# Attention denominators from partial sums and raw tiles, and quads of denominators in the linear stage

## The chip, the cores and the metric

The kernel runs on one core of a Trainium2 chip. The metric is the device time of one execution in microseconds (us); three executions of the kernel before took 5260.36, 5265.98 and 5267.3 us, a median of 5265.98.

## The reference

Two layers follow each other on an image of 512 channels and 64 x 64 points (4096 tokens).

```
# layer 0
qn = group_norm(x); vn = group_norm(qn)
q, k, v = conv1x1(qn, wq, bq), conv1x1(vn, wk, bk), conv1x1(vn, wv, bv)
attn = softmax(einsum('bhnd,bhmd->bhnm', q, k) * scale)     # 16 heads of 32
out  = conv1x1(einsum('bhnm,bhmd->bhnd', attn, v), wo, bo)
x    = (out + x) / sqrt(2)
# layer 1
qkv    = einsum('oc,bchw->bohw', w_qkv, x)
qkv_ms = concat([qkv, pointwise(depthwise5x5(qkv))])
out    = vk @ q, with vk = [v, 1] @ relu(k)^T and q = relu(q)   # 64 heads of 8, both halves
out    = out[:, :, :-1] / (out[:, :, -1:] + 1e-15)
out    = batch_norm(einsum('oc,bchw->bohw', w_proj, out)) + x
```

## The kernel before

Five stages run one after another, each a function with a program for every engine: `stage_qkv`, `stage_attention`, `stage_output`, `stage_linear` and `stage_project`. The change touches three of them.

**Attention.** A unit is one head with 1024 queries; there are 64. The 32 key tiles of a unit are taken in 16 pairs, and four pairs (eight tiles) make an octet, so that there are 256 octets. For each pair TensorE issues four score matmuls (L643), each followed by one of the matmuls of `max_product` (L630), which find the row maxima of the next unit. ScalarE exponentiates the scores into `prob` (L779), a ring of two octets; VectorE reads the maxima out of a ring of four PSUM banks (`read_max`, L806). After every second pair comes `times_v` (L656) for two older pairs. In the fourth pair of an octet, ahead of its last maximum, stands `denominators` (L666) for the octet before: matmuls with a column of ones over two sums of tiles, one result row per half and sum in a PSUM bank of the same ring. Once in a unit the maxima are turned (`transpose_shift`, L637).

The two sums of an octet come from GpSimd and VectorE. GpSimd (`eight_steps`, L606 and L612) adds tiles 0 to 3 into the first sum, and tiles 6 and 7 onto the second, whose first addition, tiles 4 and 5, is VectorE's (`add`, L825). The addition stands on VectorE ahead of the last maximum of the octet, and GpSimd waits for it. ScalarE reads the denominators (`read_den`, L745) ahead of an octet's first exponential. What orders the work is the program written out for each engine; the engines meet at semaphores alone.

**Linear stage.** A tile T is one role (K, V or Q) of one group of 128 channels; there are 12 tiles of 8 chunks, and one step s per chunk. A step multiplies by the weights into one PSUM bank (`conv1`, L1253), which ScalarE reads twice. After the eighth step comes `conv5` (L1269), a burst of 400 matmuls of 32 x 32 that makes the 5 x 5 part of four chunks; the other four come from VectorE's `dsum` (L1439, L1442), through one matmul each (`mix`, L1280). Pieces of kind "c" come from `conv1`, pieces "x" from the 5 x 5 part; the x pieces of tile T are read during tile T+1, four by `read_conv5` (four activations each, L1361) and four by `read_mix` (one activation, L1367). Each piece is then posted: K and V pieces are transposed (L1301), Q pieces are multiplied into a numerator (L1294) and into 16 denominator rows (L1296), both read by ScalarE (L1377, L1379) and stored. A Q piece is posted three steps after it is made (`LAG`). The next `conv5` waits for all x pieces of the tile before (`x_read`).

**Project stage.** It loads the denominators, inverts them on VectorE (`invert`, L1586), stores the inverses (`store_inverse`, L1501), loads them back spread over the heads (L1521), divides (L1594) and multiplies by the weights (L1549).

Of the kernel before, what the change touches and what calls it, by code (L numbers as in the profile page):

```python
# [38 lines left out]
class Scratch:  # L39


    def __init__(self, nc):
# [6 lines left out]
        self.den = nc.dram_tensor("scratch_den", (2, GROUPS, HPG, N), F32, kind="Internal").ap()  # L49
# [294 lines left out]
def stage_attention(nc, x, scr, v_tok, x1, x_in, ident_d):  # L344
# [14 lines left out]
    ADDS = 5  # L359
# [20 lines left out]
    with ExitStack() as ctx:  # L380
# [34 lines left out]
        dve_added = sem("b_dve_added")  # L415
# [12 lines left out]
        counted = (*k_in, *q_in, v_in, shift_in, scored, exped, times_v_done, dve_added, pool_added,  # L428
# [169 lines left out]
        def _(pool):  # L598
            def eight_steps(g, b):

                p = prob[:, b * OCT:(b + 1) * OCT, :]
                a_, b_ = sums[:, b, 0, :], sums[:, b, 1, :]
# [21 lines left out]
        def _(pe):  # L624
# [177 lines left out]
        def _(dve):  # L802
# [36 lines left out]
            def turn(i, final):  # L839
                for u, head, par, c in units(i):  # L840
                    place = par * UNITS + c
                    for pair in range(PAIRS):
# [6 lines left out]
                        for n in range(PER_PAIR):  # L849
                            if n == PER_PAIR - 1 and pair % (OCT // 2) == OCT // 2 - 1:  # L850
                                o = pair // (OCT // 2)
                                add(u * OCTS + o, o % 2)
# [198 lines left out]
def stage_linear(nc, w_all, dw_all, pw_all, mask_d, heads_d, ident_d, scr, x1):  # L1051

    ALONE = 4
# [5 lines left out]
    LAG = {K: 1, V: 1, Q: 3}  # L1061
    RING = 4
    OUT_RING = 4
    BLK = P // 4
# [22 lines left out]
    for s in range(STEPS):  # L1087
        for kind in "xc":
            for i in posts_at[s][kind]:
                parts = (("num", 0), ("den", 1)) if role_of(i) == Q else (("tr", 1 if kind == "x" else 0),)  # L1090
# [5 lines left out]
    final = {(kind, i): number[kind, i, "den" if role_of(i) == Q else "tr"] for kind, i in PIECES}  # L1096
    v_order = [p for s in range(STEPS) for p in times_at[s]]
    v_number = {p: n for n, p in enumerate(v_order)}
    q_order = sorted((p for p in PIECES if role_of(p[1]) == Q), key=lambda p: number[(*p, "den")])
    q_number = {p: n for n, p in enumerate(q_order)}  # L1100

# [6 lines left out]
    with ExitStack() as ctx:  # L1108
# [12 lines left out]
        bd = sb("d_bd", [P, 2, P])  # L1121
# [9 lines left out]
        den_w = sb("d_den_w", [P, 2, HPG])  # L1131
        num = sb("d_num", [P, OUT_RING, BANK])
        den = sb("d_den", [HPG, OUT_RING, BANK])
# [24 lines left out]
        stored = [sem(f"d_stored{i}") for i in range(OUT_RING)]  # L1158
        block = ctx.enter_context(nc.Block())

        @block.sync
        def _(sp):
# [16 lines left out]
            def store(kind, i):  # L1179
                q, n, at = q_number[kind, i], chunk_of(kind, i), part_of(kind)  # L1180
                r = q % OUT_RING
                sp.wait_ge(post_read, number[kind, i, "den"] + 1)
# [512 lines left out]
```

## Time and profile before

| | us |
|---|---|
| median of three runs | 5265.98 |
| the profiled execution, own time | 5261.72 |
| its span in the trace | 5259.9 |
| TensorE busy | 4970.8 (95%) |
| VectorE busy | 4297.0 (82%) |
| GpSimd busy | 3101.7 (59%) |
| ScalarE busy | 2902.8 (55%) |

The span begins with the program's first instruction and ends with its last. Attention takes it from about 336 us to 3872 us, the linear stage from 4019 to 4971 us, the project stage the rest. Busy time of TensorE counts matmuls whose ends are modelled, so that one which starts late for a wait can still look covered; the starts of the instructions are what to read.

### The profile page before, as it was taken

The page shows a single profiled execution, that of the slowest core. Times are in us where ns is not written, and L with a number is a line of the kernel's source. Part 1 is how long each engine was busy: PE and PEld are TensorE (multiplying, and loading weights), DVE is VectorE, ACT ScalarE, POOL GpSimd, SP SyncE. Part 2 cuts the span into 40 slices and gives each one's busy share as a digit, 9 for nine tenths or more (in the row PEclk, how much of TensorE's full clock was granted, in tenths as well). Part 3 has the DMA queues.
Part 4 walks back from the last instruction along what each step waited for, and adds up shares of the span by engine and source line. Part 5 has one row for each costly group of instructions (what it writes and reads, how often), then busy time and mean ns, then how long its engine had stood idle before and what let it go on. Part 6 is the DMA issues. An engine that isn't in the chain of part 4 may idle for free. (4 is left out here: it accounts for less than half of the span.)

```text
span 5259.9 us, 100067 instructions
## 1 busy us (share of the span) xinstructions
PE 4970.8 (95%) x32432; PEld 2650.2 (50%) x32432; DVE 4297.0 (82%) x5145; ACT 2902.8 (55%) x5349; POOL 3101.7 (59%) x1336
## 2 busy tenths in 40 slices
PE   7989999999999999999999999999978999999797
PEld 6854444444444444444444444444435555555343
DVE  4359999999999999999999999999946878678533
ACT  2216666666666666666666666666641443443302
POOL 0008888888888888888888888888840000000000
PEclk9979999999999999999999999999989999999998
DMA  4330000100001010010100101011031010000254
GB/s 155 128 101 12 24 17 24 28 13 24 17 24 28 14 27 14 24 29 12 29 12 24 29 12 29 12 27 61 22 126 38 16 34 16 31 25 23 94 155 155
DMA packets 103338, 221.24 MB, mean 42 GB/s; under 512 B 13776, under 2 KB 23120, under 8 KB 100176
## 3 DMA queue, kind: packets, MB, share of 16 engines
q1 hardware_dynamic: 102864, 215.00, 13.0%
q8 instruction: 288, 4.72, 0.4%
q14 instruction: 186, 1.52, 0.1%
HBM read 132.64 MB, written 81.79 MB: 41 GB/s over the span
## 5 line engine op out<-in xcount | busy, mean ns | idle before, releaser
L612 POOL TENSOR_TENSOR b_sums<-b_sums,b_prob 128x1024 f32<-128x1024 f32 x1024 | 2440.0, 2383 | 432.5 <-DVE b_sums L825 284.7
L806 DVE TENSOR_REDUCE b_mx<-b_pmax 128x1 f32<-128x512 f32 x4096 | 2504.8, 679 | 213.7 <-PE b_pmax L630 211.8
L779 ACT ACTIVATE b_prob<-b_pscore 128x512 f32<-128x512 f32 x4096 | 2174.2, 610 | 483.1 <-PE b_pscore L643 476.0
L630 PE MATMUL b_pmax<-b_kst,b_qst 96*128 96x512 f32 x4096 | 1808.3, 445 | 107.1 <-DVE b_mx L806 91.2
L643 PE MATMUL b_pscore<-b_qst,b_kst 98*128 98x512 f32 x4096 | 1636.8, 400 | 16.1 <-DMA b_qst<-b_mlow 11.8
L630 PEld LDWEIGHTS b_pmax<-b_kst,b_qst 96*128 96x128 f32 x4096 | 781.9, 191 | 1012.1 <-DVE b_mx L806 667.1
L656 PE MATMUL b_pout<-b_prob,b_vst 128*32 128x512 f32 x8192 | 991.9, 602 | 0.0
L643 PEld LDWEIGHTS b_pscore<-b_qst,b_kst 98*128 98x128 f32 x4096 | 780.5, 191 | 154.4 <-ACT b_prob L779 25.0
L606 POOL TENSOR_TENSOR b_sums<-b_prob 128x1024 f32<-128x1024 f32 x256 | 612.7, 2393 | 390.6 <-ACT b_prob L779 386.2
L825 DVE TENSOR_TENSOR b_sums<-b_prob 128x1024 f32<-128x1024 f32 x256 | 789.0, 3082 | 43.0 <-ACT b_prob L779 43.0
L1442 DVE SCALAR_TENSOR_TENSOR d_dsum<-d_ypad,d_dw,d_dsum 128x2048 f32<-128x2048 f32 x288 | 681.9, 2368 | 10.2
L656 PEld LDWEIGHTS b_pout<-b_prob,b_vst 128*32 128x32 f32 x8192 | 214.5, 109 | 487.4 <-issue 283.1
L745 ACT ACTIVATE b_outd<-b_pmax 128x512 f32<-128x512 f32 x256 | 153.2, 598 | 554.8 <-PE b_pmax L666 424.1
L1225 POOL TENSOR_TENSOR d_num_w<-d_vks,d_mask 128x128 f32<-128x128 f32 x8 | 3.6, 456 | 762.6 <-ACT d_vks L1403 762.6
L1253 PE MATMUL d_pmain<-v_tok,d_w 128*128 128x512 f32 x768 | 351.7, 601 | 17.7 <-DVE d_tv_x L1426 11.0
L1269 PE MATMUL d_pdw<-d_ypad,d_wtap 32*32 32x512 f32 x9600 | 312.9, 599 | 3.2 <-ACT d_piece_x L1367 2.4
L1361 ACT ACTIVATE d_piece_x<-d_pdw 32x512 f32<-32x512 f32 x192 | 113.0, 589 | 310.4 <-PE d_pdw L1269 307.8
L666 PE MATMUL b_pmax<-b_sums,b_ones 128*1 128x512 f32 x2048 | 266.9, 593 | 2.8 <-POOL b_sums L612 2.8
L1269 PEld LDWEIGHTS d_pdw<-d_ypad,d_wtap 32*32 32x32 f32 x9600 | 214.1, 103 | 96.4 <-issue 18.3
L1549 PE MATMUL f_ps<-f_num,f_w 128*128 128x512 f32 x512 | 223.0, 599 | 35.6 <-DVE f_num L1594 35.6
L1253 PEld LDWEIGHTS d_pmain<-v_tok,d_w 128*128 128x128 f32 x768 | 138.8, 191 | 185.4 <-issue 175.3
L1439 DVE TENSOR_SCALAR d_dsum<-d_ypad,d_dw 128x2048 f32<-128x2048 f32 x12 | 15.4, 1287 | 217.6 <-ACT d_piece_c L1354 217.6
(159 smaller groups left out, 2422.3 us busy)
## 6 DMA issues: line engine op xcount, KB each, us to landing
b_kst<-scratch_kh SPq DMA_DIRECT2D x32, 512.0 KB, 10.6
b_qst<-scratch_qh SPq DMA_DIRECT2D x128, 128.0 KB, 2.9
scratch_att<-b_outn SPq DMA_DIRECT2D x128, 128.0 KB
scratch_num<-d_num SPq DMA_DIRECT2D x64, 256.0 KB, 2.0
f_num<-scratch_num SPq DMA_DIRECT2D x8, 2048.0 KB, 10.1
f_rden<-scratch_rden SPq DMA_DIRECT2D x64, 256.0 KB, 9.5
v_tok<-in_x SPq DMA_DIRECT2D x8, 1024.0 KB, 12.7
scratch_qh<-a_high SPq DMA_DIRECT2D x8, 1024.0 KB, 4.2
```

The lines of the kernel that those rows point to most:

```text
L606: pool.tensor_tensor(a_, p[:, 0, :], p[:, 1, :], ALU.add).then_inc(pool_added, 1)
L612: pool.tensor_tensor(acc, acc, p[:, step, :], ALU.add).then_inc(pool_added, 1)
L630: pe.matmul(pmax[bank][:], qst[0:SUMS, b, t * P:(t + 1) * P], kst[0:SUMS, par, j * BANK:(j + 1) * BANK], start=True, stop=True).then_inc(m ...
L643: pe.matmul(pscore[score_bank(hs)][:], kst[0:FULL, par, kt * P:(kt + 1) * P], qst[0:FULL, b, at], start=True, stop=True).then_inc(scored, 1)
L656: mm = pe.matmul(pout[row:row + HD, :], vst[:, par, kt, :], prob[:, kt % PBUF, half * BANK:(half + 1) * BANK], start=(pair == 0), stop=(pa ...
L666: mm = pe.matmul(pmax[bank][row:row + 1, :], ones[:], sums[:, o % 2, s, half * BANK:(half + 1) * BANK], start=True, stop=True)
L779: act.activation(prob[:, kt % PBUF, half * BANK:(half + 1) * BANK], pscore[score_bank(hs)][:], ACT.Exp, scale=SCALE).then_inc(exped, 1)
L806: dve.tensor_reduce(mx[:, b, t, j:j + 1], pmax[bank][:], AX.X, ALU.max).then_inc(max_read, 1)
L825: dve.tensor_tensor(sums[:, b, 1, :], prob[:, b * OCT + 4, :], prob[:, b * OCT + 5, :], ALU.add).then_inc(dve_added, 1)
L1253: mm = pe.matmul(pmain[:], w[:, b, k, :], x1[:, k, n * BANK:(n + 1) * BANK], start=(k == 0), stop=(k == KC - 1))
L1269: mm = pe.matmul(pdw[r][c * BLK:(c + 1) * BLK, :].rearrange("p (r c) -> p r c", c=IMG), wtap[rows, b, tap, :], ypad[rows, b, y:y + ROWS, d ...
L1442: add = dve.scalar_tensor_tensor(acc, src, dw[:, b, tap:tap + 1], acc, ALU.mult, ALU.add)
```

## The change

In attention, GpSimd makes both sums alone, each of three tiles (0 to 2, 3 to 5), in four additions; tiles 6 and 7 are not added. `denominators` has eight matmuls: four over the sums, and four that accumulate the raw tiles 6 and 7 from `prob` onto the same rows. VectorE's addition is gone. In the linear stage a Q piece gives a numerator alone; after every fourth piece one bundle of four matmuls makes the denominators of all four pieces, in four strips of 32 rows of one bank. ScalarE reads them at once, VectorE inverts them there, and SyncE stores the inverses where the project stage reads them. The four `mix` matmuls of a tile become one bundle of sixteen matmuls of 32 x 32, and its results are read by `read_conv5`, in four activations each. `LAG` of Q is 2 instead of 3, the ring of pieces 6 instead of 4. The project stage has no inversion and no store of inverses.

```diff
-    ADDS = 5
+    ADDS = 4
+    RAW = 6
...
                 pool.wait_ge(den_done, done(g - 1))
-                pool.wait_ge(exped, done((g * OCT + 2) * 2))
-                pool.tensor_tensor(a_, p[:, 0, :], p[:, 1, :], ALU.add).then_inc(pool_added, 1)
-                for n, (acc, step) in enumerate(((a_, 2), (a_, 3), (b_, 6), (b_, 7))):
-                    pool.wait_ge(pool_added, done(g * ADDS + n + 1))
-                    pool.wait_ge(exped, done((g * OCT + step + 1) * 2))
-                    if n == 2:
-                        pool.wait_ge(dve_added, done(g + 1))
-                    pool.tensor_tensor(acc, acc, p[:, step, :], ALU.add).then_inc(pool_added, 1)
+                for s in range(2):
+                    at = 3 * s
+                    pool.wait_ge(exped, done((g * OCT + at + 2) * 2))
+                    pool.tensor_tensor(sums[:, b, s, :], p[:, at, :], p[:, at + 1, :], ALU.add).then_inc(pool_added, 1)
+                    pool.wait_ge(pool_added, done(g * ADDS + 2 * s + 1))
+                    pool.wait_ge(exped, done((g * OCT + at + 3) * 2))
+                    pool.tensor_tensor(sums[:, b, s, :], sums[:, b, s, :], p[:, at + 2, :],
+                                       ALU.add).then_inc(pool_added, 1)
...
                 pe.wait_ge(pool_added, done((u * OCTS + o + 1) * ADDS))
-                for half in range(2):
-                    for s in range(2):
-                        row = (half * 2 + s) * HD
-                        mm = pe.matmul(pmax[bank][row:row + 1, :], ones[:],
-                                       sums[:, o % 2, s, half * BANK:(half + 1) * BANK],
-                                       start=True, stop=True)
+                pe.wait_ge(exped, done((u * OCTS + o + 1) * OCT * 2))
+                for raw in range(2):
+                    for half in range(2):
+                        for s in range(2):
+                            row = (half * 2 + s) * HD
+                            terms = prob[:, o % 2 * OCT + RAW + s, :] if raw else sums[:, o % 2, s, :]
+                            mm = pe.matmul(pmax[bank][row:row + 1, :], ones[:],
+                                           terms[:, half * BANK:(half + 1) * BANK],
+                                           start=(raw == 0), stop=(raw == 1))
                 mm.then_inc(den_done, 1)
...
-            def add(g, b):
-
-                dve.wait_ge(den_done, done(g - 1))
-                dve.wait_ge(exped, done((g * OCT + 6) * 2))
-                dve.tensor_tensor(sums[:, b, 1, :], prob[:, b * OCT + 4, :], prob[:, b * OCT + 5, :],
-                                  ALU.add).then_inc(dve_added, 1)
...
-    LAG = {K: 1, V: 1, Q: 3}
-    RING = 4
+    LAG = {K: 1, V: 1, Q: 2}
+    RING = 6
...
+            def store_quad(kind, i):
+                q, at = quad_number[kind, i], part_of(kind)
+                row = (at * GROUPS + group_of(i)) * HPG
+                sp.wait_ge(inverted, q + 1)
+                for c in range(QUAD):
+                    n = chunk_of(kind, i - QUAD + 1 + c)
+                    sp.dma_start(scr.rden[row:row + HPG, n * BANK:(n + 1) * BANK],
+                                 den[c * BLK:c * BLK + HPG, q % 2, :]).then_inc(den_stored[q % 2], 16)
...
-                pe.matmul(pdw[n][:], bd[:, T % 2, :], dsum[:, T % 2, n * BANK:(n + 1) * BANK],
-                          start=True, stop=True).then_inc(l_done, 1)
+                for r in range(4):
+                    rows = slice(r * BLK, (r + 1) * BLK)
+                    for c in range(ALONE):
+                        mm = pe.matmul(pdw[r][c * BLK:(c + 1) * BLK, :], bdq[rows, b, :],
+                                       dsum[rows, b, c * BANK:(c + 1) * BANK], start=True, stop=True)
+                mm.then_inc(l_done, 1)
...
-                    free(number[kind, i, "den"])
-                    pe.matmul(ppost[1][0:HPG, :], den_w[:, at, :], mine, start=True, stop=True).then_inc(post_done, 1)
+                    if i % QUAD == QUAD - 1:
+                        free(number[kind, i, "den"])
+                        for c in range(QUAD):
+                            mm = pe.matmul(ppost[1][c * BLK:(c + 1) * BLK, :], den_w[:, at, :],
+                                           piece[kind][:, (i - QUAD + 1 + c) % RING, :], start=True, stop=True)
+                        mm.then_inc(post_done, 1)
...
-                c = i % CHUNKS
-                act.wait_ge(burst_done, i // CHUNKS + 1)
+                c = i % SUPER
+                if i % CHUNKS < SUPER:
+                    act.wait_ge(burst_done, i // CHUNKS + 1)
+                else:
+                    act.wait_ge(l_done, i // CHUNKS + 1)
                 out = slot("x", i)
                 for r in range(4):
                     last = act.activation(out[r * BLK:(r + 1) * BLK, :], pdw[r][c * BLK:(c + 1) * BLK, :], func(i))
                 last.then_inc(x_read, 1)
...
-                act.activation(slot("x", i), pdw[n][:], func(i)).then_inc(x_read, 1)
...
+            def invert(kind, i):
+                dve.wait_ge(post_read, number[kind, i, "den"] + 1)
+                at = den[:, quad_number[kind, i] % 2, :]
+                dve.reciprocal(at, at).then_inc(inverted, 1)
...
-                dve.reciprocal(dens[:, 1, at], dens[:, 0, at]).then_inc(inverted, 1)
```

TensorE in attention, at the end of an octet (`b_pout` are the values, `b_pmax` the ring of maxima and denominators), before and then with the change:

```order
L643 MATMUL b_pscore<-b_qst,b_kst 128x512
L656 MATMUL b_pout<-b_prob,b_vst 32x512 x8
L666 MATMUL b_pmax<-b_sums,b_ones 1x512 x4
L630 MATMUL b_pmax<-b_kst,b_qst 128x512
L643 MATMUL b_pscore<-b_qst,b_kst 128x512
```

```order
L642 MATMUL b_pscore<-b_qst,b_kst 128x512
L655 MATMUL b_pout<-b_prob,b_vst 32x512 x8
L668 MATMUL b_pmax<-b_sums,b_ones 1x512 x4
L668 MATMUL b_pmax<-b_prob,b_ones 1x512 x4
L629 MATMUL b_pmax<-b_kst,b_qst 128x512
L642 MATMUL b_pscore<-b_qst,b_kst 128x512
```

Four matmuls over `prob` stand behind the four over `b_sums`; nothing else has moved there.

VectorE in attention, at the same place (`b_mx` takes the maxima), before; with the change the middle three rows are absent and the reads follow each other:

```order
L805 REGISTER_ALU
L806 TENSOR_REDUCE b_mx<-b_pmax 128x1
L823 REGISTER_ALU
L824 ISA
L825 TENSOR_TENSOR b_sums<-b_prob 128x1024
L805 REGISTER_ALU
L806 TENSOR_REDUCE b_mx<-b_pmax 128x1
```

TensorE in the linear stage, two steps of a Q tile and what stands at their ends (`d_pmain` is `conv1`, `d_pvk` the values times keys, `d_pdw` with `d_dsum` the mix), before and then with the change:

```order
L1253 MATMUL d_pmain<-v_tok,d_w 128x512 x4
L1313 MATMUL d_pvk<-d_tv_x,d_tk 128x129 x4
L1301 MATMUL d_ppost<-d_ident,d_piece_x 128x128 x4
L1280 MATMUL d_pdw<-d_dsum,d_bd 128x512
L1294 MATMUL d_ppost<-d_piece_c,d_num_w 128x512
L1296 MATMUL d_ppost<-d_piece_c,d_den_w 16x512
L1269 MATMUL d_pdw<-d_ypad,d_wtap 32x512 x400
```

```order
L1308 MATMUL d_pdw<-d_dsum,d_bdq 32x512 x16
L1323 MATMUL d_ppost<-d_piece_c,d_num_w 128x512
L1279 MATMUL d_pmain<-v_tok,d_w 128x512 x4
L1346 MATMUL d_pvk<-d_tv_x,d_tk 128x129 x4
L1334 MATMUL d_ppost<-d_ident,d_piece_x 128x128 x4
L1323 MATMUL d_ppost<-d_piece_c,d_num_w 128x512
L1327 MATMUL d_ppost<-d_piece_c,d_den_w 32x512 x4
L1279 MATMUL d_pmain<-v_tok,d_w 128x512 x4
```

The first piece shows the last step of a tile, in which mix and denominator stand between the transposes and the burst. In the second, the mix of a whole tile stands in its fifth step, the denominators of four pieces in the sixth; the last step has neither.

## Rows read from the trace of the kernel before

**Rows 1.** Busy time by stretch: PE, PEld, DVE, ACT, POOL; then PEclk, DMA share, GB/s.

```profile
1000.00:2000.00 1000.00, 970.35 (x5304) 489.02 (x5307) 938.70 (x1286) 681.80 (x1290) 872.46 (x368) 1.00 0.08 22
3836.00:3850.00 14.00, 13.27 (x60) 4.19 (x56) 3.69 (x2) 8.54 (x17) 13.18 (x6) 0.87 0.00 1
4200.00:4973.00 773.00, 758.66 (x9709) 416.22 (x9708) 565.15 (x243) 323.08 (x575) 45.11 (x41) 1.00 0.09 29
```

**Rows 2.** Timeline of TensorE, one unit of attention (start us, us, engine, line, names, count).

```profile
2014.30 1.04 PE L666 MATMUL b_pmax<-b_sums,b_ones 128*1 128x512 f32 x8
...
2040.84 1.04 PE L666 MATMUL b_pmax<-b_sums,b_ones 128*1 128x512 f32 x8
2041.81 0.50 PE L630 MATMUL b_pmax<-b_kst,b_qst 96*128 96x512 f32 x1
...
2046.84 1.92 PE L656 MATMUL b_pout<-b_prob,b_vst 128*32 128x512 f32 x16
2048.70 0.50 PE L630 MATMUL b_pmax<-b_kst,b_qst 96*128 96x512 f32 x1
...
2052.62 1.92 PE L656 MATMUL b_pout<-b_prob,b_vst 128*32 128x512 f32 x16
2054.36 1.04 PE L666 MATMUL b_pmax<-b_sums,b_ones 128*1 128x512 f32 x8
...
2062.34 0.50 PE L630 MATMUL b_pmax<-b_kst,b_qst 96*128 96x512 f32 x1
...
2066.93 1.92 PE L656 MATMUL b_pout<-b_prob,b_vst 128*32 128x512 f32 x16
2068.67 1.04 PE L666 MATMUL b_pmax<-b_sums,b_ones 128*1 128x512 f32 x8
```

**Rows 3.** Timeline of VectorE in the octet that begins at 2040.84.

```profile
2040.50 3.24 DVE L825 TENSOR_TENSOR b_sums<-b_prob 128x1024 f32<-128x1024 f32 x1
...
2049.24 4.88 DVE L806 TENSOR_REDUCE b_mx<-b_pmax 128x1 f32<-128x512 f32 x8 [0.71 <-PE b_pmax L630]
```

**Rows 4.** Costliest groups: VectorE's and GpSimd's sums, scores, the 5 x 5 burst.

```profile
L825 DVE TENSOR_TENSOR b_sums<-b_prob 128x1024 f32<-128x1024 f32 x256 | 789.0, 3082 | 43.0 <-ACT b_prob L779 43.0
L612 POOL TENSOR_TENSOR b_sums<-b_sums,b_prob 128x1024 f32<-128x1024 f32 x1024 | 2440.0, 2383 | 432.5 <-DVE b_sums L825 284.7
L643 PE MATMUL b_pscore<-b_qst,b_kst 98*128 98x512 f32 x4096 | 1636.8, 400 | 16.1 <-DMA b_qst<-b_mlow 11.8
L1269 PE MATMUL d_pdw<-d_ypad,d_wtap 32*32 32x512 f32 x9600 | 312.9, 599 | 3.2 <-ACT d_piece_x L1367 2.4
```

**Rows 5.** Timeline of TensorE, linear stage, last step of a Q tile: mix, numerator, denominator, burst.

```profile
4440.18 1.02 PE L1280 MATMUL d_pdw<-d_dsum,d_bd 128*128 128x512 f32 x2
4441.03 1.02 PE L1294 MATMUL d_ppost<-d_piece_c,d_num_w 128*128 128x512 f32 x2
4441.99 1.03 PE L1296 MATMUL d_ppost<-d_piece_c,d_den_w 128*16 128x512 f32 x2
4442.95 1.13 PE L1269 MATMUL d_pdw<-d_ypad,d_wtap 32*32 32x512 f32 x31
```

**Rows 6.** Timeline of ScalarE in that step: the V piece read.

```profile
4440.38 0.60 ACT L1396 ACTIVATE d_tv_x<-d_ppost 128x512 f32<-128x512 f32 x1 [0.24 <-PE d_ppost L1301]
```

**Rows 7.** Timeline of ScalarE in an earlier step of that tile: a 5 x 5 piece read.

```profile
4396.83 2.39 ACT L1361 ACTIVATE d_piece_x<-d_pdw 32x512 f32<-32x512 f32 x4
```

**Rows 8.** Chain of waits at the start of the project stage.

```profile
4973.86 2.81 DMA f_proj<-scratch_den
4976.70 3.36 DVE f_proj L1586
4980.08 9.69 DMA scratch_rden<-f_proj
```

**Rows 9.** DMA issues of the numerators (count, KB each, median us to landing).

```profile
f_num<-scratch_num SPq DMA_DIRECT2D x8, 2048.0 KB, 10.1
```

More of the change, by code:

```diff
@@ L1095, in stage_linear, with inverted_before @@
                     latest[bank] = n
-    final = {(kind, i): number[kind, i, "den" if role_of(i) == Q else "tr"] for kind, i in PIECES}
+    final = {(kind, i): number[kind, i // QUAD * QUAD + QUAD - 1, "den"] if role_of(i) == Q
+             else number[kind, i, "tr"] for kind, i in PIECES}
     v_order = [p for s in range(STEPS) for p in times_at[s]]
     v_number = {p: n for n, p in enumerate(v_order)}
-    q_order = sorted((p for p in PIECES if role_of(p[1]) == Q), key=lambda p: number[(*p, "den")])
+    q_order = sorted((p for p in PIECES if role_of(p[1]) == Q), key=lambda p: number[(*p, "num")])
     q_number = {p: n for n, p in enumerate(q_order)}
+    quads = [p for p in q_order if p[1] % QUAD == QUAD - 1]
+    quad_number = {p: n for n, p in enumerate(quads)}
+    def inverted_before(kind, i):
+        return min(main_step(kind, i) // CHUNKS + 1, TILES)
+    quads_before = {T: [p for p in quads if inverted_before(*p) == T] for T in range(TILES + 1)}
+    quads_after = {T * CHUNKS + ALONE: quads_before[T] for T in range(TILES)}
+    quads_after[TILES * CHUNKS + ALONE] = [p for p in quads_before[TILES] if p[0] == "c"]
+    quads_after[STEPS] = [p for p in quads_before[TILES] if p[0] == "x"]
     def group_of(i):
@@ L1158, in stage_linear @@
         stored = [sem(f"d_stored{i}") for i in range(OUT_RING)]
+        den_stored = [sem(f"d_den_stored{i}") for i in range(2)]
+        inverted = sem("d_inverted")
         block = ctx.enter_context(nc.Block())
@@ L1193, in _ @@
                     load(T + 1)
+                for p in quads_after.get(s, ()):
+                    store_quad(*p)
                 for kind in "xc":
@@ L1197, in _ @@
                             store(kind, i)
+            for p in quads_after[STEPS]:
+                store_quad(*p)
             for r in range(OUT_RING):
-                sp.wait_ge(stored[r], len(range(r, len(q_order), OUT_RING)) * 32)
+                sp.wait_ge(stored[r], len(range(r, len(q_order), OUT_RING)) * 16)
+            for r in range(2):
+                sp.wait_ge(den_stored[r], len(range(r, len(quads), 2)) * 16 * QUAD)
         @block.gpsimd
@@ L1324, in _ @@
                 x = s - CHUNKS
-                if 0 <= x < LAST and x % CHUNKS >= SUPER:
-                    mix(x)
+                if 0 <= x < LAST and x % CHUNKS == SUPER:
+                    mix(x // CHUNKS)
                 for i in posts_at[s]["c"]:
@@ L1422, in _ @@
         def _(dve):
+            dve.memset(den_w[:], 0.0).then_inc(zeroed, 1)
             for b in range(2):
@@ L1443, in _ @@
                     add.then_inc(dlink, 1)
+            for p in quads_before[TILES]:
+                invert(*p)
 def stage_project(nc, wprojT, chan_bn, scr, x1, out):
@@ L1472, in stage_project @@
         ps = [ctx.enter_context(nc.psum_tensor(f"f_ps{i}", [P, BANK], F32)) for i in range(8)]
-        den_in = [sem(f"f_den_in{i}") for i in range(2)]
-        inverted = sem("f_inverted")
-        inv_out = [sem(f"f_inv_out{i}") for i in range(2)]
         w_in = sem("f_w_in")
@@ L1496, in _, with turn @@
                 sp.sem_inc(s, CREDIT)
[L1498 to L1504 removed]
             sp.dma_start(w[:], wprojT.rearrange("(m p) o -> p m o", p=P)).then_inc(w_in, 16)
             sp.dma_start(par[:], chan_bn).then_inc(w_in, 16)
[L1507 removed]
+            def turn(i):
                 for b in range(2):
@@ L1522, in turn @@
                                          .to_broadcast([HPG, GH, BANK])).then_inc(rden_in[part], 16)
-                    if not final:
-                        store_inverse(n + 2, b)
-            store_inverse(0, 0)
-            store_inverse(1, 1)
-            with sp.Fori(0, CHUNKS // 2 - 1) as i:
-                turn(i, False)
-            turn(CHUNKS // 2 - 1, True)
+            with sp.Fori(0, CHUNKS // 2) as i:
+                turn(i)
             for t in range(KC):
```

80 lines of the change are left out of this document (31 added, 49 removed).

## Prediction

> **What bounds the kernel now.** I read the busy time by stretch first, since the share over the whole span mixes stages. In attention TensorE is busy 970 of 1000 us and VectorE 939, ScalarE only 682 [rows 1]: two engines are nearly full, and the page does not tell which waits for which. The timeline of TensorE tells it [rows 2]. An octet has two runs of sixteen score and maximum matmuls. The second goes from 2048.70 to 2052.62, 3.92 us; the first, of the same instructions, from 2041.81 to 2046.84, 5.03 us. On VectorE its addition runs from 2040.50 for 3.24 us [rows 3]: no maximum is read meanwhile, the ring of four banks fills, and TensorE stands. Behind the second run VectorE had been idle 0.71 us and reads eight maxima in 4.88 us [rows 3], slower than TensorE's 3.92, but the ring carries the lag and the matmuls behind the run (1.86 us or more) let it catch up.
>
> So without the addition TensorE's own octet is 3.92 + 1.86 (2046.84 to 2048.70) + 3.92 + 1.74 (2052.62 to 2054.36) + 0.97 (2040.84 to 2041.81, denominators) = 12.41 us. The run with the turn takes 4.59 instead of 3.92 (2062.34 to 2066.93), since the turn takes a bank of the ring; I count those 0.67 us as staying. A unit is 4 x 12.41 + 0.67 = 50.31 us of TensorE's own. It took 54.37 (2014.30 to 2068.67) [rows 2]. **4.06 us a unit are stalls from VectorE's addition.**
>
> In the linear stage TensorE goes from instruction to instruction [rows 5], except where ScalarE is late; the project stage starts behind a chain of transfers [rows 8].
>
> **The change, part by part.**
>
> *VectorE's addition goes.* It is 256 x 3.08 us [rows 4], but on the path it is worth the stalls alone: -4.06 us a unit, if all go. VectorE then needs two times 4.88 us for an octet's maxima, some 10 us with the turn's small reads, against 13.3 of TensorE (below). What is late next is TensorE itself.
>
> *Four more denominator matmuls an octet.* They are of the same form as the four that stand there, in the same four strips. No row shows eight in a row; the bounds are 0.86 us, half of the 1.74 that two groups of `times_v` take, and 0.97, what a denominator group takes with the change back to scores [rows 2]. That change comes once an octet whatever the group's length, so 0.86 is nearest: +3.44 us a unit. TensorE's octet becomes 13.27 us. The new wait for all exponentials of the older octet is for work that ended four pairs earlier. ScalarE reads denominators 0.86 us later relative to the last run, but the next scores come later by as much; it is busy 682 of 1000 us and gets no more to do [rows 1].
>
> *GpSimd* goes from five additions to four, 4 x 2.38 [rows 4], under 10.2 us with its gaps, and no longer waits for VectorE. It is covered by TensorE's 13.27.
>
> *A rule that speaks against this.* An addition costs VectorE 3.08 us and GpSimd 2.38 [rows 4]. The Trainium skill (GPSIMD Engine Reference, Engine selection) would put an elementwise addition on VectorE, GpSimd being about two times slower with two inputs. The trace differs: run beside GpSimd's, VectorE's addition is the dearer one, and the measurement decides. By the rule the addition would take VectorE some 1.2 us, an estimate from its factor and the 2.38; most of the stall would have another cause and stay, and the time would be that of rival A.
>
> Over the 63 units that have maxima, -4.06 + 3.44 = -0.62 gives **-39 us**. The last unit has none and no such stall: four groups of 0.86 us, **+3**. The scores wait 11.8 us in all for a row of shifts that is loaded [rows 4], at units' starts, right behind a denominator group; a group 0.86 us longer hides part, between 0 and 7 us; I take **-4**.
>
> *Linear stage, TensorE.* A denominator takes 0.96 us, a mix 0.85 [rows 5]. Of 64 denominators 53 lie ahead of the last burst, and become 13 bundles; a bundle is four matmuls in four strips, bounded by 0.86 and by 0.97 as above; I take 0.96: -40 x 0.96 = -38. Of 48 mixes 44 become 11 bundles of 16 matmuls, 32 instructions at the burst's 312.9/9600 us [rows 4], 1.04: -44 x 0.85 + 11 x 1.04 = -26.
>
> *Given back in the last step of a tile.* The burst waits until the last x piece is read. Today that read is one activation behind a short mix, done by the time numerator and denominator are through: the burst starts at 4442.95 [rows 5]. Now it is four activations, 2.39 us [rows 7]. ScalarE begins the V piece at 4440.38 [rows 6], can begin the four 0.5 us later, ends them at 4443.3, and the burst starts near 4443.4; TensorE, without mix and denominator, would be through at 4441.1. That is 2.2 us of wait here, 2.6 to 2.9 in K and V tiles, which have less to do on TensorE there; between 0 (were ScalarE ahead) and 2.9. I take 2.6, eleven times: +29. The other steps hold: ScalarE is busy 323 of 773 us there [rows 1], and 144 more activations less 48 denominator reads, at 0.6 us (2.39/4), make that 381.
>
> VectorE's sixteen inversions, 3.36 us each [rows 8], two at a tile's start, fall into its waits: it is busy 565 of the 773 us [rows 1], with them some 620 of 735. Were that cover gone, they would cost up to 54 us. The part after the last burst is bound by ScalarE; it loses eight denominator reads and gains a last inversion and four stores: -3, between -8 and +4. Linear stage: -38 - 26 + 29 - 3 = **-38 us**.
>
> *Project stage.* Load, inversion and store of the first inverses go, 2.81 + 3.36 + 9.69 = 15.9 us [rows 8], the most that can be won. Under them lay the weights (2 MB) and the first numerators (2 MB, 10.1 us to land [rows 9]); now these stand in the open. If both must land one after the other, some 20 us from the same start, about 5 us are won. I take the middle, **-10 us**.
>
> **Sum.** -39 + 3 - 4 - 38 - 10 = -88. Against the profiled execution's own 5261.7 us that is 5174. The median of the three runs stands 4.3 us above that execution; I let this lie within the range.
>
> **The rivals.**
>
> *A. The maxima still hold TensorE: slower.* VectorE reads a maximum in 0.61 us (4.88/8), TensorE makes one in 0.47; if the first run stays behind the second's pace even without the addition, for instance because the ring is one bank short while denominators lie in it longer, part of the 4.06 us stays while the 3.44 are paid in full. It decides at a third: if more than 1.4 us (88/63) a unit stay, nothing is won in the whole kernel. With half staying, +128: 5302 us. For it: the turn's run is held by just that, one bank less. Against it: the second run follows 1.86 us behind the first, and shows no stall. 8 in 100, and 3 more for a third staying (5259).
>
> *B. The clock.* In an octet of the last unit the granted clock is 0.87 of 2.4 GHz instead of 1.00 [rows 1], in a stretch where TensorE stands idle between short pieces: part of it ran at 1.2 GHz. Should the longer stretch of denominators, which fill one column in 32 of the array, do that to every octet, 0.13 x 14 = 1.8 us come on top each time, 466 in all: 5640. Against it: the present group and the bursts of the linear stage keep the clock at 1.00 [rows 1], and idle time falls. 3 in 100.
>
> *C. The linear stage gives nothing,* because ScalarE, with 144 more activations, binds its other steps as well: 5212, still faster. For it: a burst already waits for it. Against it: half its time there is idle. 9 in 100.
>
> *D. More is won:* the turn's 0.67 us go too (-42), or the burst does not wait (-29): about 5120. 7 in 100.
>
> **How the numbers follow.** The forecast as summed has 70 in 100, and lies within 5135 to 5215 by the bounds of its terms (28 us for 0.97 instead of 0.86 in attention, 8 in the linear stage, 6 in the project stage, up to 29 if bursts do not wait). With C, and part of D and of A's milder case, the range is 5130 to 5230. A difference under 0.2% (10.5 us) is about what a measurement of this kernel cannot tell from none. Faster by more than that: the forecast, C and D, 86; slower: A with half staying and B, 11; between: A's milder case, 3.
>
> **What would show it.** Right: no addition on VectorE in attention, runs of 3.9 us in both halves of an octet, octets of 13.3 us, units near 53.8, GpSimd idle over a fifth of attention, granted clock 1.00; sixteen inversions in the linear stage; bursts waiting for a read of 5 x 5 pieces by ScalarE; the first division about 10 us earlier after the stage begins. Wrong: first runs above 4.2 us (A), a granted clock under 0.95 in attention (B), steps of the linear stage that wait for ScalarE elsewhere (C). A unit above 54.4 us would refute the core.

## The result and the profile after

The changed kernel takes 5228.33 us (median of three, 5226.27 to 5231.29) against 5265.98: ratio 0.9929, interval 0.9915 to 0.9942. It is faster, by 37.7 us where 92 (against that median) were forecast; inside the stated range, by 1.7 us, but 54 us short of the forecast. The profiled execution has 5231.29 us of its own and a span of 5229.4, 30.5 us under the span before. Where these went, from the same marks in both traces (first score, last attention matmul, first and last burst, first projection matmul):

| stretch | before | after | change | forecast |
|---|---|---|---|---|
| start to the first score | 381.4 | 380.9 | -0.5 | 0 |
| attention, to its last matmul on TensorE | 3490.6 | 3478.9 | -11.7 | -40 |
| to the first 5 x 5 burst | 187.6 | 191.4 | +3.8 | 0 |
| first burst to the end of the last | 877.7 | 854.0 | -23.7 | -35 |
| to the first projection matmul | 68.3 | 71.2 | +2.8 | -13 |
| to the end | 254.3 | 253.0 | -1.3 | 0 |

**Attention did what was said, in most of its units.** Busy time by stretch of the changed kernel (us, then PE, PEld, DVE, ACT, POOL; granted clock; DMA):

```profile
1000.00:2000.00 1000.00, 996.92 (x5902) 525.86 (x5895) 722.80 (x1210) 655.27 (x1289) 695.85 (x294) 0.99 0.08 22
4200.00:4900.00 700.00, 663.57 (x9684) 393.22 (x9666) 581.73 (x246) 337.94 (x594) 35.27 (x30) 0.99 0.08 26
```

VectorE falls from 939 to 723 of 1000 us and GpSimd is idle for 304; TensorE goes from 970 to 997 [rows 1]. TensorE's timeline of one octet:

```profile
2010.56 1.04 PE L668 MATMUL b_pmax<-b_prob,b_ones 128*1 128x512 f32 x8
2011.53 0.50 PE L629 MATMUL b_pmax<-b_kst,b_qst 96*128 96x512 f32 x1
...
2015.47 1.92 PE L655 MATMUL b_pout<-b_prob,b_vst 128*32 128x512 f32 x16
2017.33 0.50 PE L629 MATMUL b_pmax<-b_kst,b_qst 96*128 96x512 f32 x1
...
2021.27 1.92 PE L655 MATMUL b_pout<-b_prob,b_vst 128*32 128x512 f32 x16
2023.01 1.04 PE L668 MATMUL b_pmax<-b_sums,b_ones 128*1 128x512 f32 x8
2023.86 1.04 PE L668 MATMUL b_pmax<-b_prob,b_ones 128*1 128x512 f32 x8
2024.84 0.50 PE L629 MATMUL b_pmax<-b_kst,b_qst 96*128 96x512 f32 x1
```

The first run of sixteen (2011.53 to 2015.47) and the second (2017.33 to 2021.27) now take 3.94 us each, where the first had taken 5.03 [rows 2]. Eight denominator matmuls take 0.85 + 0.98. From one denominator group to the next it is 13.31 us, forecast 13.27. VectorE waits for TensorE ahead of every run instead of the reverse; its timeline there:

```profile
2012.07 4.88 DVE L808 TENSOR_REDUCE b_mx<-b_pmax 128x1 f32<-128x512 f32 x8 [2.86 <-PE b_pmax L629]
2017.87 4.88 DVE L808 TENSOR_REDUCE b_mx<-b_pmax 128x1 f32<-128x512 f32 x8 [0.92 <-PE b_pmax L629]
```

The median of 62 units, taken from the starts of their first denominator group, falls from 54.36 to 53.90 us (53.75 forecast).

**But one unit in eight does not.** The program loops over eight units. At six of its seven turns TensorE waits, and its clock halves behind some of the waits. TensorE's timeline at the second turn, and its busy time and granted clock (the number behind the count) in windows around it:

```profile
1244.55 1.04 PE L668 MATMUL b_pmax<-b_sums,b_ones 128*1 128x512 f32 x8
1245.40 1.04 PE L668 MATMUL b_pmax<-b_prob,b_ones 128*1 128x512 f32 x8
1246.38 0.49 PE L629 MATMUL b_pmax<-b_kst,b_qst 96*128 96x512 f32 x1
1248.03 0.49 PE L642 MATMUL b_pscore<-b_qst,b_kst 98*128 98x512 f32 x1 [1.16 <-DMA b_qst<-b_mlow]
```

```profile
1233.00:1238.00 5.00, 5.00 (x31) 1.00 0.01 3
1243.00:1248.00 5.00, 3.87 (x33) 1.00 0.05 11
1248.00:1253.00 5.00, 4.97 (x14) 0.67 0.03 8
1253.00:1258.00 5.00, 5.00 (x23) 0.65 0.00 0
```

The row of shifts lands late at this turn (a DMA), and TensorE stands 1.16 us; in the ten us from 1248 on the granted clock is 0.67 and 0.65, so part of them ran at 1.2 GHz. Of seven turn units the three with such a stretch behind the wait took 57.6 to 58.9 us, three without it 56.1 to 56.3, and one, the last, had no wait. Not every wait is for the row. TensorE's waits from 420 to 3790 us (us, times, longest; "issue" is a wait for no engine and no transfer that the profile shows):

```profile
PE b_pscore L642 <- issue: 5.0, 3, 1.9
PE b_pscore L642 <- DMA b_qst<-b_mlow: 2.5, 2, 1.4
PE b_pmax L629 <- DVE b_mx L808: 1.9, 1, 1.9
```

All six stand at turns. In the kernel before the turns cost as much (seven turn units together 19.0 us over the median), but the units right behind them were 13.0 us under it, 52.3 us instead of 54.4. There the denominator groups behind the second turn stand 12.45 and 12.67 us apart, where those ahead of it stand 13.55 apart; 12.45 is close to the 12.41 that the prediction had worked out as TensorE's own octet:

```profile
1222.42 1.04 PE L666 MATMUL b_pmax<-b_sums,b_ones 128*1 128x512 f32 x8
1235.97 1.04 PE L666 MATMUL b_pmax<-b_sums,b_ones 128*1 128x512 f32 x8
...
1268.15 1.04 PE L666 MATMUL b_pmax<-b_sums,b_ones 128*1 128x512 f32 x8
1280.60 1.04 PE L666 MATMUL b_pmax<-b_sums,b_ones 128*1 128x512 f32 x8
1293.27 1.04 PE L666 MATMUL b_pmax<-b_sums,b_ones 128*1 128x512 f32 x8
```

VectorE's additions there took 1.21 and 2.36 us, not 3.26 as in the median. So most of the addition's stall is absent for two octets, and the turn is in part made up. In the changed kernel the turn units are 20.0 us over their median and those behind them 0.3 over: nothing is made up.

**The linear stage has new waits.** TensorE's waits from the first burst to the end of the last, in the changed kernel, then before (us, times, longest):

```profile
PE d_pdw L1295 <- ACT d_piece_x L1397: 25.8, 11, 2.8
PE d_ppost L1334 <- ACT d_num L1408: 13.3, 15, 0.9
PE d_ppost L1334 <- ACT d_den L1414: 2.4, 3, 0.8
```

```profile
PE d_ppost L1301 <- ACT d_den L1379: 4.6, 6, 0.8
PE d_pdw L1269 <- ACT d_piece_x L1367: 2.4, 7, 0.3
```

The first line is the forecast wait for the last 5 x 5 piece; the second was not forecast. In the last step of a K tile, where x pieces of the Q tile before it are still to be multiplied (TensorE, then ScalarE):

```profile
4499.98 1.02 PE L1323 MATMUL d_ppost<-d_piece_x,d_num_w 128*128 128x512 f32 x2
4501.90 0.63 PE L1334 MATMUL d_ppost<-d_ident,d_piece_c 128*128 128x128 f32 x4 [0.90 <-ACT d_num L1408]
4504.33 2.25 PE L1295 MATMUL d_pdw<-d_ypad,d_wtap 32*32 32x512 f32 x58 [1.80 <-ACT d_piece_x L1397]
```

```profile
4501.15 0.60 ACT L1408 ACTIVATE d_num<-d_ppost 128x512 f32<-128x512 f32 x1
4501.78 2.40 ACT L1397 ACTIVATE d_piece_x<-d_pdw 32x512 f32<-32x512 f32 x4
```

A numerator (L1323) is followed by transposes (L1334) that use the same PSUM bank, so they wait until ScalarE has read it. Before, a denominator matmul of 0.96 us in the other bank stood between the two [rows 5]. And behind four of the burst waits the clock halved again. The burst of 800 matmuls with and without it, behind the same wait:

```profile
4122.62 27.62 PE L1295 MATMUL d_pdw<-d_ypad,d_wtap 32*32 32x512 f32 x800 [2.77 <-ACT d_piece_x L1397]
...
4579.04 26.08 PE L1295 MATMUL d_pdw<-d_ypad,d_wtap 32*32 32x512 f32 x800 [2.77 <-ACT d_piece_x L1397]
```

### The profile page after: what moved, and what is told of

Read it like the earlier page. It is cut to its first block and busy times, and to the rows that moved or that the text cites. A ratio compares the mean times of both kernels' runs of the same rounds, so it can differ in the third digit from the quotient of the medians.

```text
span 5229.4 us, 103029 instructions
## 1 busy us (share of the span) xinstructions
PE 4989.3 (95%) x34768; PEld 2766.3 (53%) x34768; DVE 3575.3 (68%) x4898; ACT 2878.2 (55%) x5445; POOL 2477.0 (47%) x1068
## 5 line engine op out<-in xcount | busy, mean ns | idle before, releaser
L781 ACT ACTIVATE b_prob<-b_pscore 128x512 f32<-128x512 f32 x4096 | 2089.8, 619 | 350.1 <-PE b_pscore L642 345.0
L607 POOL TENSOR_TENSOR b_sums<-b_prob 128x1024 f32<-128x1024 f32 x512 | 1220.7, 2384 | 1332.5 <-ACT b_prob L781 1332.5
L629 PE MATMUL b_pmax<-b_kst,b_qst 96*128 96x512 f32 x4096 | 1716.0, 422 | 17.9 <-DMA b_qst<-scratch_ql 15.2
L610 POOL TENSOR_TENSOR b_sums<-b_sums,b_prob 128x1024 f32<-128x1024 f32 x512 | 1220.5, 2384 | 89.7 <-POOL b_sums L607 86.7
L1397 ACT ACTIVATE d_piece_x<-d_pdw 32x512 f32<-32x512 f32 x384 | 226.3, 589 | 327.0 <-PE d_pdw L1295 313.9
L1295 PE MATMUL d_pdw<-d_ypad,d_wtap 32*32 32x512 f32 x9600 | 319.1, 610 | 26.7 <-ACT d_piece_x L1397 25.8
L668 PE MATMUL b_pmax<-b_prob,b_ones 128*1 128x512 f32 x2048 | 266.5, 592 | 0.0
L1577 PEld LDWEIGHTS f_ps<-f_num,f_w 128*128 128x128 f32 x512 | 98.0, 192 | 159.3 <-issue 159.3
```

Source lines behind the costliest of these rows:

```text
L607: pool.tensor_tensor(sums[:, b, s, :], p[:, at, :], p[:, at + 1, :], ALU.add).then_inc(pool_added, 1)
L610: pool.tensor_tensor(sums[:, b, s, :], sums[:, b, s, :], p[:, at + 2, :], ALU.add).then_inc(pool_added, 1)
L629: pe.matmul(pmax[bank][:], qst[0:SUMS, b, t * P:(t + 1) * P], kst[0:SUMS, par, j * BANK:(j + 1) * BANK], start=True, stop=True).then_inc(m ...
L668: mm = pe.matmul(pmax[bank][row:row + 1, :], ones[:], terms[:, half * BANK:(half + 1) * BANK], start=(raw == 0), stop=(raw == 1))
L781: act.activation(prob[:, kt % PBUF, half * BANK:(half + 1) * BANK], pscore[score_bank(hs)][:], ACT.Exp, scale=SCALE).then_inc(exped, 1)
L1295: mm = pe.matmul(pdw[r][c * BLK:(c + 1) * BLK, :].rearrange("p (r c) -> p r c", c=IMG), wtap[rows, b, tap, :], ypad[rows, b, y:y + ROWS, d ...
```

## Experiments

All times are medians; each was run beside the kernel before on the same chip (5263 to 5266 us).

**The two halves apart.** One kernel has `stage_attention` of the change and all else as before, the other the reverse.

```diff
-    ADDS = 5
+    ADDS = 4
+    RAW = 6
...
```

```diff
-    LAG = {K: 1, V: 1, Q: 3}
-    RING = 4
+    LAG = {K: 1, V: 1, Q: 2}
+    RING = 6
+    QUAD = 4
...
```

> The kernel before with the attention part of the change alone. By the prediction on record attention gains 40 us: about 5226 us. By the new theory (TensorE is now the bound of every unit, so the waits for the row of shifts at the loop's turns, one unit in eight, and the half clock behind them are paid in full, where the kernel before made them up in the next unit): units of 53.9 us, but 2 to 5 us more at a turn, 12 us won in all: about 5254 us.

> The changed kernel with attention as before, so the linear and project parts alone. By the prediction on record 48 us are won: about 5218 us. By the new theory about 20: the twelve bursts span 24 us less, the part behind the last burst takes 8 us more because numerators that follow each other in one bank each wait for ScalarE's read, the start of the project stage 5 us less: about 5246 us.

Measured: 5247.72 us (ratio 0.9970, 0.9959 to 0.9982), 16 won, near the new theory's 12 and far from 40; and 5235.40 us (0.9949, 0.9936 to 0.9963), 28 won, between the two. Both halves fell short, and attention by more.

**What the four matmuls cost, and who holds TensorE.**

```diff
-                for raw in range(2):
+                for raw in range(1):
...
-                                           start=(raw == 0), stop=(raw == 1))
+                                           start=True, stop=True)
```

> The changed kernel with the four denominator matmuls over unsummed tiles left out (tiles 6 and 7 of each octet are then not in the denominator). If TensorE alone sets the pace and four matmuls cost 0.86 us, a unit takes 53.87 - 3.44 = 50.4 us, attention 220 us less: about 5008 us. If the ring of maxima and VectorE's reads still hold TensorE (rival A of the prediction), a unit stays above 51.5 us: above 5075 us.

Measured: 5011.24 us, as the first theory said (this kernel leaves tiles 6 and 7 out of the denominators). The median unit is 50.47 us, 3.43 under the changed kernel's 53.90, so a group of four costs 0.86 us, the figure taken; and 50.47 is close to the 50.31 us that the prediction had worked out as TensorE's own. Rival A is refuted: without the addition TensorE's waits for VectorE come to 2.7 us in the whole of attention. The turn units are 17.4 us over the median here too.

**The turn of the loop.** The same edit in the changed kernel and in the kernel before:

```diff
-    EARLY = 2
+    EARLY = 3
```

> The changed kernel with the shifts made three pairs of key tiles before a unit's end instead of two, so that the row is loaded some 3 us earlier. By the new theory the waits of 1.2 to 1.9 us at the loop's turns and the half clock behind them go: 15 to 21 us less than the changed kernel, about 5210 us. By its rival (TensorE is late at the turn for its own instructions, and the row is only the last thing named) nothing changes: 5228 us.

> The kernel before with the shifts made three pairs before a unit's end instead of two, the same edit that took 20 us off the changed kernel. By the theory of lost slack the unit behind a loop's turn made up most of what the turn cost (52.3 us instead of 54.4), so little is to be won: 0 to 8 us, about 5260 us. By its rival (the edit is worth the same wherever TensorE waits at a turn) 15 to 20 us: about 5246 us.

Measured: 5208.18 us in the changed kernel, 20 under it; 5260.32 us in the kernel before (ratio 0.9997, 0.9988 to 1.0006), no change that can be told. The same edit is worth 20 us where TensorE is the bound, and nothing that can be told where VectorE's addition paced it. How slack absorbs it can be read in the kernel before: with the edit the median octet with the turn of the shifts takes 14.13 us instead of 14.30, and the next one 13.02 instead of 12.88. The new theory was wrong in one respect. TensorE's waits in attention (420 to 3790 us) with the edit:

```profile
PE b_pscore L642 <- issue: 5.0, 5, 1.2
PE b_pmax L629 <- DVE b_mx L808: 4.2, 6, 2.0
```

The wait for the row is gone, but waits for no engine and no transfer ("issue", 5.0 us before the edit too) stay at the turns, and reads of maxima come late behind them. Six turn units are still 2.2 to 3.9 us over the median: of the 18.9 us that attention gains, the turns give 5.0 (two of the three stretches at 1.2 GHz are gone). The most, 11.8, is the median unit, 53.71 instead of 53.90 us, because the octet with the turn of the shifts takes 13.80 instead of 13.96; which no theory had held. What remains of the theory is what the pair of runs shows, that the kernel before absorbed the edit. What holds TensorE at the turn stays open.

**Who is late at the burst.** ScalarE's reads of the mixed pieces but the first move to the head of a step, under the convolution's matmuls:

```diff
-                if 0 <= x < LAST and x % CHUNKS < SUPER:
+                if 0 <= x < LAST and x % CHUNKS != SUPER:
                     read_conv5(x)
...
-                if 0 <= x < LAST and x % CHUNKS >= SUPER:
+                if 0 <= x < LAST and x % CHUNKS == SUPER:
                     read_conv5(x)
```

> The changed kernel with the last three of the four mixed x pieces of a tile read by ScalarE at the head of a step, under the convolution's matmuls, instead of behind the step's other reads. If the order of ScalarE's reads in a tile's last step is what the burst waits for, the 25.8 us of waits go and with them the half clock behind some of them (four times 3.4 us): 26 to 33 us less, about 5199 us. If ScalarE is short of time in that step whatever its order, half of it at most: about 5215 us.

Measured: 5207.41 us, 21 won. First burst to the end of the last takes 832.4 us instead of 854.0, and no burst waits for a piece and no clock halves there any more. The 25.8 us of waits and 6 us of half clock are gone, and 10.8 come back in other waits, these and 2.3 us more for reads of values:

```profile
PE d_ppost L1334 <- ACT d_num L1408: 17.9, 18, 1.5
PE d_pmain L1279 <- ACT d_piece_c L1387: 4.9, 6, 1.0
```

**Numerators in two banks.**

```diff
-                    parts = (("num", 0), ("den", 1))
+                    parts = (("num", int(kind == "x")), ("den", int(kind == "c")))
...
-                    pe.matmul(ppost[0][:], num_w[:, at, :], mine, start=True, stop=True)
+                    pe.matmul(ppost[int(kind == "x")][:], num_w[:, at, :], mine, start=True, stop=True)
...
```

> The changed kernel with numerators of x pieces in the second bank and those of c pieces in the first (denominators in the other one each time), so that a numerator is no longer followed in its own bank by the next transposes or numerator of the same step. If the missing denominators had kept these apart, the 13.3 us of waits of transposes for numerators go, and the 8 us that the part behind the last burst took more: 15 to 21 us less, about 5210 us. If ScalarE's reads set the pace there whatever the bank, at most 5 us: 5224 us.

Measured: 5220.94 us (ratio 0.9920, 0.9907 to 0.9934), 7 won: nearer to the rival, and hardly clear of noise, since the changed kernel's interval is 0.9915 to 0.9942. The waits of transposes for numerators are gone, but TensorE only comes sooner to the burst:

```profile
PE d_pdw L1295 <- ACT d_piece_x L1397: 29.1, 11, 2.9
```

That line stood at 25.8 before the edit; a granted clock under 1.00 in the burst, four times in the changed kernel, comes seven times. So the shared bank was the cause of these waits, but behind them stood the same late reads. The part behind the last burst went from 71.2 to 69.8 us only, so the bank does not explain its lengthening.

**All three, and the last tile.** One kernel has the three edits above together (shifts earlier, reads first, two banks); in the other the last tile's reads stay in the old order:

```diff
-                if 0 <= x < LAST and x % CHUNKS != SUPER:
+                last = x // CHUNKS == TILES - 1
+                if 0 <= x < LAST and (x % CHUNKS < SUPER or x % CHUNKS > SUPER and not last):
                     read_conv5(x)
...
```

> The changed kernel with all three: shifts a pair earlier, the three pieces read at the head of a step, numerators in two banks. If the three losses are separate, the sum of their gains, 20 + 29 + 18 = 67 us: about 5161 us. If they cover each other in the linear stage (ScalarE is late at the burst anyway), about 5180 us.

> The kernel with all three edits, but with the last tile's mixed pieces read behind the step's other reads as in the changed kernel. If reading them at the head of the step holds numerators back once no convolution runs beside it (3.7 us at most ahead of one numerator), the part behind the last burst takes 2 to 3 us less: about 5176 us. Otherwise 5179 us, as with all three.

Measured: 5179.28 us, 49 under the changed kernel: the sum of what the three edits won one by one (20, 21 and 7), and less than the 67 that had been expected of them; and 5176.45 us, the part behind the last burst 71.4 us instead of 73.5 (the two times lie within each other's spread, so the stretch has to tell).

**The merged mixes undone.** Four mixes a tile with one read each, as before; quads of denominators stay.

```diff
-                        mm = pe.matmul(pdw[r][c * BLK:(c + 1) * BLK, :], bdq[rows, b, :],
-                                       dsum[rows, b, c * BANK:(c + 1) * BANK], start=True, stop=True)
+                pe.matmul(pdw[n][:], bd[:, T % 2, :], dsum[:, T % 2, n * BANK:(n + 1) * BANK],
+                          start=True, stop=True).then_inc(l_done, 1)
...
-    OUT_RING = 4
+    OUT_RING = 3
```

> The changed kernel with the four mixes of a tile as before, one matmul group and one read by ScalarE each (the ring of numerators has three places instead of four, for want of room). By the terms of the prediction TensorE gets 26 us more to do and the bursts wait 29 us less, with some 7 us of half clock behind them and 7 us of ScalarE's reads behind the last burst: 5211 to 5225 us, so the merging by itself wins nothing. If the waits ahead of the bursts have another cause than the fourfold reads, the 26 us come on top: 5254 us.

> Shifts a pair earlier, numerators in two banks, and the four mixes separate as before, read behind the step's other reads (ring of numerators of three places). Against the kernel with all three edits TensorE has 26 us more of mixes and ScalarE 7 us less behind the last burst, and no burst waits in either: about 5198 us. If the fourfold reads still cost the kernel with all three edits as much as the merging wins, 5179 us.

Measured: 5209.75 us, 19 under the changed kernel, a little better than expected: the merging by itself loses. From first burst to the end of the last it takes 842.7 us (854.0 merged), and from there to the projection 65.4 (71.2), 17 us for the two. TensorE's waits between the bursts:

```profile
PE d_ppost L1332 <- ACT d_num L1408: 8.1, 9, 0.9
...
PE d_pdw L1297 <- ACT d_piece_x L1398: 1.4, 4, 0.3
```

The burst's wait is 1.4 us in all. With the other two edits it takes 5182.72 us, between the two expectations: merged mixes with reads at the head of the step (5176.45) are better by 6 us, not by 20.

**The last tile alone.** All three edits and the last tile's reads in the old order, with that tile's four mixes separate.

```diff
-                if 0 <= x < LAST and x % CHUNKS == SUPER:
+                if 0 <= x < LAST - CHUNKS and x % CHUNKS == SUPER:
                     mix(x // CHUNKS)
+                if LAST - CHUNKS <= x < LAST and x % CHUNKS >= SUPER:
+                    mix_last(x % CHUNKS - SUPER)
```

> The kernel with all three edits and the last tile's reads in the old order, and that last tile's four mixes separate with one read each, as all tiles had them before; the other eleven stay merged. If the fourfold reads of those four pieces (1.8 us more each) lengthen the part behind the last burst, it takes 65.5 us from the last burst to the projection instead of 71.4, as in the kernel with all mixes separate, and the time is 5170 us. If what ends that part is the last inversion and its stores, it stays at 5176 us.

Measured: 5171.94 us (ratio 0.9828, 0.9814 to 0.9841), as expected; behind the last burst 64.1 us instead of 71.4. Of these 7.3 us 6.3 are ScalarE's last read, which comes sooner (four times the 1.8 us that a fourfold read takes more than one would be 7.2), and 1.0 is the start of the project stage. ScalarE's timeline there, a piece with four reads, then one with one:

```profile
4864.02 2.40 ACT L1414 ACTIVATE d_piece_x<-d_pdw 32x512 f32<-32x512 f32 x4
...
4870.97 0.60 ACT L1410 ACTIVATE d_piece_x<-d_pdw 128x512 f32<-128x512 f32 x1 [1.11 <-PE d_pdw L1320]
```

It is the fastest kernel of the study, 56 us under the changed one and 92 under the kernel before, what had been forecast for the change itself.

## Why the prediction was wrong

*The core held.* The stalls of VectorE's addition are gone (4.06 us a unit), eight denominator matmuls cost what was said, the clock of 1000 us of attention is 0.99, so rival B fell, and GpSimd has time left. Of the signs listed, the runs, the octet and the sixteen inversions came true, the bursts waited 25.8 us (29 forecast), and the first division came 8.8 us sooner after the stage's start. (One reading was a little off: in rival A a maximum costs TensorE 0.49 us, 3.92/8, not 0.47.) Without the four matmuls a unit takes 50.47 us, so the stall went whole, and the addition was its cause. What made it dear stands in the trace of the kernel before, by its line (shortest, median and longest in ns), then GpSimd's addition beside the one of VectorE in [rows 3], then an addition of VectorE with GpSimd idle:

```profile
L825 DVE TENSOR_TENSOR b_sums<-b_prob x256: 1214/3262/3401, 394.0 to 3860.5; 128x1024 f32<-128x1024 f32 x128
```

```profile
2040.28 2.37 POOL L612 TENSOR_TENSOR b_sums<-b_sums,b_prob 128x1024 f32<-128x1024 f32 x1 [0.17 <-POOL b_sums L612]
```

```profile
1267.80 1.21 DVE L825 TENSOR_TENSOR b_sums<-b_prob 128x1024 f32<-128x1024 f32 x1
```

VectorE's addition of [rows 3] began 0.22 us behind GpSimd's and ended 1.09 us behind its end. So it is with 252 of the 256: each begins while an addition of GpSimd runs, and ends 1.08 or 1.09 us after that one. The other four found GpSimd idle and took 1.21 or 1.22 us. In the last unit the reverse is seen too: five additions of GpSimd overlapped one of VectorE and took 3.1 us instead of 2.38. The Trainium skill (SBUF — State Buffer, Who interferes with whom) says that a VectorE instruction with two SBUF inputs and a GpSimd instruction that reads SBUF exclude each other. This trace agrees. The factor of two between the engines that the prediction took from the Trainium skill (GPSIMD Engine Reference, Engine selection) holds for the undisturbed additions, 1.21 against 2.38 us. What failed is the step from there to a stall with another cause: VectorE's addition ran without one of GpSimd's in 4 cases of 256.

*First failing step: "-4.06 us a unit, if all go", as a gain over 63 units with "-4" for the row of shifts.* It priced the stall for an even row of units. The four us a unit were also the slack in which a turn's lateness was made up (13.0 of 19.0 us). With them gone the turns are paid in full: 14.4 us that no term held (20.0 + 0.3 against 19.0 - 13.0). The forecast even took the row's wait as shrinking. That slack absorbs such differences the runs with the shifts a pair earlier show: 20 us in the changed kernel, no change that can be told in the kernel before. Why TensorE is late at a turn at all stays open. Of attention's 28 missing us 10 more are the median unit (0.46 us won in 62 units, not 0.62 in 63; four octets of 13.30 to 13.31 us instead of 13.27), and 3 lie in a few other units. Of the 11.7 us won, some 3 were worth nothing: the last denominator group had waited 2.85 us for GpSimd in the kernel before, beside the way of the outputs to memory (the next stage's first load comes 9.5 us after their store is issued, 9.2 with the change), and the next stretch is 3.8 us longer; what the last 0.9 of it is was not looked for.

*Second: "The other steps hold", in the linear stage.* The sum of TensorE's work, -64, was right, and ScalarE has time to spare on the average. The denominators had a second use: they stood between a numerator and the next user of its bank. Forecast for the bursts' stretch -38 - 26 + 29 = -35; the trace adds 11 (13.3 + 2.4 of waits in place of 4.6) and four half-clock stretches at 1.5 us, 6, and takes 6 off for the burst waits (25.8 in place of 2.4, so 23 more and not 29): some -24, where -23.7 was measured. Rival C had named the mechanism, ScalarE binding the other steps, but at the price of everything.

*Third: "it loses eight denominator reads and gains a last inversion and four stores: -3".* It left out the four mixed pieces behind the last burst, read fourfold: 7.2 us by its own rows, and in the last experiment 6.3 up to ScalarE's last read. From the burst's end that read comes 37.5 us later (33.3 before), and from there to the project stage's first load 7.4 us pass instead of 3.3, the inversion and its stores. Together +8.2. Part of it is neither. Of the 4.1 us up to the last read ScalarE is busy for 1.9; the rest is waiting for TensorE. TensorE stood 4.1 us for two preparations on GpSimd, which run beside VectorE's `dsum` and take 3.8 us; before, with VectorE idle, they took 0.8:

```profile
4911.52 1.46 POOL L1250 TENSOR_TENSOR d_num_w<-d_vks,d_mask 128x128 f32<-128x128 f32 x1 [66.65 <-ACT d_vks L1438]
4912.97 2.36 POOL L1251 TENSOR_SCALAR d_den_w<-d_hmask,d_vks 128x16 f32<-128x16 f32 x1
```

And behind that wait TensorE's granted clock is 0.53 from 4915 to 4925 us, then 0.50 from 4933 to 4948 us, so that a numerator takes 2.05 us instead of 1.02; in the kernel before it was 1.00 up to ScalarE's last read. No run took these two apart.

*Fourth: the project stage, "-10, the middle".* The lower bound, about 5, was right: -5.4 (31.7 us before, 26.3 after). TensorE starts on the second division, not the first, and its inverses take 14.27 us to land:

```profile
4959.64 14.27 DMA f_rden<-scratch_rden
4973.93 2.31 DVE f_num L1616
```

So the merging was the change's weak part, and a loss of some 17 us in the kernel as it stood: by its two terms alone (-26 + 29) it was worth nothing, and the half clock behind the burst waits and the reads behind the last burst came on top.

## What to carry to other kernels

Before a stall is booked as gain, look at what else it pays for: units that follow a hiccup and run faster than the median show that the stall is slack, and the hiccup will cost its full size once another engine is the bound. An instruction that is removed may have been the spacing between two users of one buffer; look at what becomes its neighbour. An instruction may be dear for what runs beside it: compare its shortest time with its median before moving it. And when a producer's matmuls are merged at the cost of more reads, put the reads where their engine idles: moving three reads to the head of a step won 21 us, the whole change to attention 16.

## What the hardware showed

In the turns and bursts of the changed kernel TensorE's clock fell to 1.2 GHz behind waits of only 1.2 to 2.8 us, and not each time: of the two bursts shown above behind waits of 2.77 us one took 27.62 us, at a granted clock of 0.94, and the other 26.08, at 1.00. In this profile that is 1.5 us at each of four bursts and 1.4 to 2.8 at each of three turns, some 13 us in all, which another execution need not have. So a wait on TensorE can cost more than itself.

At the second turn the second row of shifts was issued at 1243.66 us and TensorE could go on at 1248.03; a unit earlier the same issue, at 1189.80, was in time. Instruction transfers lie beside the late one. Their DMA queues from 1238 to 1252 us (packets, MB, share):

```profile
q8 instruction: 3, 0.05, 1.5%
q14 instruction: 4, 0.03, 0.6%
```

That they delay the row was not tried.
